# A graph layer and a feed-forward layer on one core: the second phase written out, and a new order of work where the phases meet

## The reference, cut to what matters

```python
# x: 10000 x 1024, src, dst: 5000 edges
xn   = layernorm(x)
h    = xn @ W.T + b
deg  = 1 + count(src)
out1 = x + deg**-.5 * sum over row's edges of deg[dst]**-.5 * h[dst]   # and the row itself
z    = layernorm(out1)
base = z @ base_W.T + base_b
low  = (z @ shared_A.T) @ shared_B.T
gate = softmax(z @ router_W.T + router_b); the top 2 of 6, normed to sum 1
low += sum over experts of gate_e * (z @ routed_A[e].T) @ routed_B[e].T     # rank 16
out  = out1 + base + low
```

## Time and profile before

| | |
|---|---|
| median of 3 runs | 2042.78 us (2038.26 to 2043.79) |
| the profiled execution, its time | 2044.74 us |
| the profiled execution, its span | 2043.0 us |
| busy: PE, DVE, POOL, ACT | 95%, 72%, 46%, 44% of the span |
| mean granted TensorE clock | 0.987 |

### The profile page before, as it was taken

The page is one execution under the profiler, slowest core; times in us unless marked ns, Lnnn a source line. Parts: engine busy times, 40 slices in busy tenths (PEclk is TensorE's granted clock), DMA queues, the critical chain, the costliest instruction groups (busy, mean ns, idle before and its releaser), DMA issues.

```text
span 2043.0 us, 31611 instructions
## 1 busy us (share of the span) xinstructions
PE 1935.7 (95%) x9583; PEld 1613.6 (79%) x9583; DVE 1466.5 (72%) x3526; ACT 908.7 (44%) x1533; POOL 937.5 (46%) x964
## 2 busy tenths in 40 slices
PE   7999999999999999947999999999999999999999
PEld 6778777777787888836878878788888878888887
DVE  6878888888776777755666767677767767776775
ACT  4455555555555555534333333333334333343342
POOL 1712444444424500146555555555555555555550
PEclk9999999999999999979999999999999999999999
DMA  6524455455444453474323333333333333333321
GB/s 245 213 101 153 163 187 175 160 185 179 160 151 144 148 166 145 155 248 118 82 73 102 105 82 95 91 98 104 103 82 92 102 87 100 103 101 84 94 60 61
DMA packets 148959, 260.20 MB, mean 127 GB/s; under 512 B 56077, under 2 KB 75357, under 8 KB 148822
## 3 DMA queue, kind: packets, MB, share of 16 engines
q1 hardware_dynamic: 99478, 237.85, 33.2%
q0 software_dynamic: 49344, 20.85, 8.0%
HBM read 273.80 MB, written 129.74 MB: 198 GB/s over the span
## 4 chain that ended last, share of the span: by engine, by line
issue 35%; PE 28%; POOL 21%; DVE 10%; ACT 2%; DMA 2%; POOLq 0%; DVEq 0%; SPq 0%; ACTq 0%
POOL acc L863 8%; PE bo L1537 4%; PE bo L1541 4%; PE bo L1539 4%; POOL piece L832 2%; POOL counted L799 2%; PE bo L1397 2%; PE bo L1401 2%; PE bo L1399 2%; POOL xpw L741 2%; POOL pw L948 2%; POOL counts L813 2%; POOL slots L820 2%; DVE acc L2161 2%; POOL tick_pool L716 1%
## 5 line engine op out<-in xcount | busy, mean ns | idle before, releaser
L863 POOL DMA_INDIRECT acc<-h_rows,row_now x312 | 505.5, 1620 | 111.6 <-issue 111.1
L1397 PE MATMUL bo<-wr_hi,left_hi 128*128 128x512 f32 x1008 | 400.1, 397 | 4.5 <-ACT bo L1149 3.1
L1401 PE MATMUL bo<-wr_hi,left_lo 128*128 128x512 f32 x1008 | 394.0, 391 | 0.0
L1399 PE MATMUL bo<-wr_lo,left_hi 128*128 128x512 f32 x1008 | 393.4, 390 | 0.0
L741 POOL TENSOR_TENSOR xpw<-xpin,neg_half 128x1 f32<-128x1 f32 x79 | 72.6, 919 | 491.5 <-DVE xpin L1705 491.5
L1537 PE MATMUL bo<-wr_hi,sum_hi 128*128 128x512 f32 x624 | 249.2, 399 | 9.2 <-DVE acc L2161 7.2
L1539 PE MATMUL bo<-wr_lo,sum_hi 128*128 128x512 f32 x624 | 244.5, 392 | 0.0
L1541 PE MATMUL bo<-wr_hi,sum_lo 128*128 128x512 f32 x624 | 244.2, 391 | 0.0
L1397 PEld LDWEIGHTS bo<-wr_hi,left_hi 128*128 128x128 f32 x1008 | 189.8, 188 | 42.6 <-issue 5.7
L1401 PEld LDWEIGHTS bo<-wr_hi,left_lo 128*128 128x128 f32 x1008 | 189.7, 188 | 40.1
L1399 PEld LDWEIGHTS bo<-wr_lo,left_hi 128*128 128x128 f32 x1008 | 190.0, 189 | 37.1
(11 more groups left out here) (231 smaller groups left out, 4275.8 us busy)
## 6 DMA issues: line engine op xcount, KB each, us to landing
xn<-x SPq DMA_DIRECT2D x79, 512.0 KB, 3.9
r_rows<-xn SPq DMA_DIRECT2D x79, 512.0 KB, 2.6
acc<-r_rows SPq DMA_DIRECT2D x79, 512.0 KB, 4.4
out<-acc SPq DMA_DIRECT2D x79, 512.0 KB
h_rows<-hrow SPq DMA_DIRECT2D x144, 256.0 KB, 3.9
acc<-h_rows,row_now POOLq DMA_INDIRECT x312
wr_raw<-w_t SPq DMA_DIRECT2D x16, 256.0 KB, 6.1
piece<-base_t SPq DMA_DIRECT2D x64, 64.0 KB, 2.8
```

Source lines behind the costliest of these rows:

```text
L863: nc.gpsimd.indirect_dma_start(to[:], None, h_dram, bass.IndirectOffsetOnAxis(ap=at, axis=0), bounds_check=NPAD - 1, oob_is_err=False, com ...
L1397: nc.tensor.matmul(ps, left_hi[n][:, k, :], wr_hi[n][:, k, :], start=False, stop=False, skip_group_check=True)
L1399: nc.tensor.matmul(ps, left_hi[n][:, k, :], wr_lo[n][:, k, :], start=False, stop=False, skip_group_check=True)
L1401: last = nc.tensor.matmul(ps, left_lo[n][:, k, :], wr_hi[n][:, k, :], start=False, stop=(k == 3), skip_group_check=True)
```

## The change

1. `pipeline` loses its loop: all 39 pairs are straight-line code on every engine.
2. GpSimd's `step`: `power(1,1)` first, then rounds (3,0), (2,3), (3,1), `power(2,0)`, (3,2); round (2,2) of the first pair goes ahead of the loop. Before: (2,2), power, (2,3), (3,0), power, (3,1).
3. At the seam, tiles 1 and 2 are filled by two chains: rounds 0 and 2 add into `acc`, rounds 1 and 3 go to a buffer `g_side` of their own, which VectorE adds before the statistics (`add_side`). Two memsets of `g_side` are new.
4. VectorE's lower parts of T1, B21, B22 move from ahead of the narrow weights' to places among the first tiles' steps; those of the low rows, T2, T3 and T4 shift too. ScalarE's high parts follow; the narrow one comes first.
5. In phase one `begin_second(0)` goes ahead of a norm and of `weigh(6)`, and T1's lower part behind the statistics of the first pair's second tile.
6. Some semaphores are merged (`zeroed`, `slots_set`), and waits on counts follow.

```diff
-SPLIT_AT = {B11: 4, T1: 8, B21: 12, B22: 16, "narrow": 17, "low": 18, "step": 19, T2: 23, T3: 27,
+SPLIT_AT = {B11: 4, "narrow": 5, T1: 9, B21: 13, "low": 14, B22: 18, "step": 19, T2: 23, T3: 27,
...
-def pipeline(eng, body, last):
-    a = DEEP
-    b = (PAIRS2 - 3) // DEEP * DEEP
-    for i in range(0, a):
-        body(Pair(i // DEEP, i % DEEP))
-    with eng.Fori(a // DEEP, b // DEEP) as k:
-        for q in range(DEEP):
-            body(Pair(k, q))
-    for i in range(b, last + 1):
+def pipeline(body, last):
+    for i in range(last + 1):
         body(Pair(i // DEEP, i % DEEP))
...
+        g_side = [sb(f"g_side{t}", [P, D], F32, w_end + 16 * HALF + 32 * HALF * t)
+                  for t in range(2)]
...
             for q in range(2):
                 nc.gpsimd.memset(g[q][:], 0.0).then_inc(g_zeroed, 1)
-            pool.wait_ge(g_zeroed, 3)
+            pool.wait_ge(done, product_at(PAIRS - 1, S3))
+            for t in range(2):
+                nc.gpsimd.memset(g_side[t][:], 0.0).then_inc(g_zeroed, 1)
+            pool.wait_ge(g_zeroed, 5)
...
+            def put_aside(t, r, at):
+
+                nc.gpsimd.indirect_dma_start(
+                    g_side[t][:], None, h_dram, bass.IndirectOffsetOnAxis(ap=at, axis=0),
+                    bounds_check=NPAD - 1, oob_is_err=False).then_inc(g_aside[t], 16)
...
             for t in range(2):
-                fill(0, t, 0, 0)
+                add_tile(z0, 0, t, 0, g_fill[t])
+                put_aside(t, 1, slot_of(t, 1))
             power(0)
             for t in range(2):
-                fill(0, t, 1, 32 + t)
-            for r in range(2, ROUNDS):
-                for t in range(2):
-                    fill(0, t, r, 30 + 2 * r + t)
-            power(1)
-            rest_in(z0, 1)
+                pool.wait_ge(g_fill[t], 16)
+                carry_wait(32 + 2 * t)
+                add_tile(z0, 0, t, 2, g_fill[t])
+                pool.wait_ge(g_aside[t], 16)
+                carry_wait(33 + 2 * t)
+                add_rows(g_side[t], slot_of(t, 3), g_aside[t])
+            rest_in(z0, 1)
+            carry_wait(36)
+            for t in range(2):
+                add_tile(z0, 1, t, 0, g_fill[t])
+            power(1)
...
+            round_of(z0, 2, 2, 48)
+
             def step(s):
                 c = 22 + 4 * (s.q % 2)
-                if s.has(2):
-                    added(s, 2, 1)
-                    carry_wait(c)
-                    add_pair(s, 2, 2)
                 if s.has(1):
                     power(s.tile(1, 1))
...
                     slots_of(s, 3)
                     rest_in(s, 3)
-                    carry_wait(c + 2)
-                    add_pair(s, 3, 0)
+                    round_of(s, 3, 0, c)
+                if s.has(2):
+                    round_of(s, 2, 3, c + 1)
+                if s.has(3):
+                    round_of(s, 3, 1, c + 2)
                 if s.has(2):
                     power(s.tile(2, 0))
                 if s.has(3):
-                    added(s, 3, 0)
-                    carry_wait(c + 3)
-                    add_pair(s, 3, 1)
+                    round_of(s, 3, 2, c + 3)
...
             sums_high(0)
+            begin_second(0)
             normalise(first(1))
             weigh(HEAD - 1)
-            begin_second(0)
...
-                if t == 5:
+                if t == HEAD - 1:
                     quarter_low(T1, wr_raw[T1], 4)
-                if t == HEAD - 1:
                     left_low(0, A11, a11[:])
...
-            right_low(T1)
-            right_low(B21)
-            right_low(B22)
             dve.wait_ge(rest_hi_ok, SPLIT_AT["narrow"])
...
             add_first()
             acc_statistics(0, 0)
             acc_scales(0)
-            low_rows_split()
+            right_low(T1)
             for v, n in ((0, A11), (1, A12)):
                 y_low(-1, n, bt[v][:])
-            z0 = Pair(0, 0)
-            right_low(T2)
+            right_low(B21)
+            low_rows_split()
+            add_side(0)
             pair_statistics(z0, 0, 0)
             acc_scales(1)
+            right_low(B22)
             choose(-1, 1)
             hidden(-1, 1)
+            y_low(0, A11, y11[:])
+            add_side(1)
             pair_statistics(z0, 0, 1)
             acc_scales(2)
-            y_low(0, A11, y11[:])
             hidden_low(-1, 1)
+            split_low("step", slice(2, 3))
+            right_low(T2)
             sums2(0, None)
             weighed_sum(0, 0, 0, first_bank[1][:], (low_done, 1))
             lows(0)
+            y_low(0, S2, y_raw[S2])
+            y_low(0, S3, y_raw[S3])
             weighed_sum(0, 0, 1, third_bank[1][:], (low_done, 2))
+            right_low(T3)
             pair_statistics(z0, 1, 0)
-            y_low(0, S2, y_raw[S2])
             acc_scales(3)
-            y_low(0, S3, y_raw[S3])
-            right_low(T3)
...
                 hidden(p, 2)
+                weighed_sum(s.acc(0, 1), s.tile(0, 1), 1, third_bank[q][:],
+                            (y_done, y_product_at(p, S1)))
                 if not s.has(-1):
                     right_low(T4)
-                weighed_sum(s.acc(0, 1), s.tile(0, 1), 1, third_bank[q][:],
-                            (y_done, y_product_at(p, S1)))
```

More of the change, by code:

```diff
@@ L393, in gnn_ffn @@
         g_fill = [sem(f"g_fill{t}") for t in range(2)]
+        g_aside = [sem(f"g_aside{t}") for t in range(2)]
         piece_in, piece_ok, piece_out = sem("piece_in"), sem("piece_ok"), sem("piece_out")
@@ L704, in _ @@
             load_right(T4)
-            pipeline(sp, step, PAIRS2)
+            pipeline(step, PAIRS2)
             for q in range(DEEP):
@@ L951, in _, with fill, slot_of @@
             z0 = Pair(0, 0)
[L952 to L958 removed]
+            def fill(t, r, n):
+                pool.wait_ge(g_fill[t], 16 * (2 + r))
+                carry_wait(n)
+                add_tile(z0, 1, t, r, g_fill[t])
+            def put_aside(t, r, at):
+                nc.gpsimd.indirect_dma_start(
+                    g_side[t][:], None, h_dram, bass.IndirectOffsetOnAxis(ap=at, axis=0),
+                    bounds_check=NPAD - 1, oob_is_err=False).then_inc(g_aside[t], 16)
+            def slot_of(t, r):
+                n = t * ROUNDS + r
+                return row_now[0][:, n:n + 1]
             carry_wait(14)
@@ L1272, in _ @@
                 .then_inc(rest_hi_ok, 1)
-            act.wait_ge(bl_step_ok, 1)
-            nc.scalar.activation(bl_hi[:, 2, :], bl_raw[:, 2, :], ACT.Copy).then_inc(rest_hi_ok, 1)
             def norm(n, a, *waits):
@@ L1341, in _ @@
                 y_high(-1, n, bt[v][:], (za_done, v + 1))
-            right_high(T2)
+            right_high(B22)
             act.wait_ge(y_done, 1)
             nc.scalar.activation(third_bank[1][:], first_bank[1][:], ACT.Copy).then_inc(y_begun, 1)
+            act.wait_ge(bl_step_ok, 1)
+            nc.scalar.activation(bl_hi[:, 2, :], bl_raw[:, 2, :], ACT.Copy).then_inc(rest_hi_ok, 1)
+            right_high(T2)
             narrow_out(-1, 1)
@@ L1375, in step @@
                     begin_second2(s.pair(1), s.mod(1, 2))
-            pipeline(act, step, PAIRS2 - 1)
+            pipeline(step, PAIRS2 - 1)
         @block.tensor
@@ L1685, in step @@
                 low(third_bank[q][:], 0, 1)
-            pipeline(pe, step, PAIRS2 - 1)
+            pipeline(step, PAIRS2 - 1)
         @block.vector
@@ L2074, in pair_statistics @@
                 if s.filled(a):
-                    dve.wait_ge(g_fill[t], 16 * ROUNDS * (s.pair(a) + 1))
+                    dve.wait_ge(g_fill[t], 16 * (2 + ROUNDS * s.pair(a)))
                 else:
@@ L2202, in low_rows_split, with add_side @@
                                         ALU.subtract).then_inc(bl_step_ok, 1)
-                for n, at in (("low", slice(0, 2)), ("step", slice(2, 3))):
-                    dve.wait_ge(rest_hi_ok, SPLIT_AT[n])
-                    dve.wait_ge(bl_step_ok, 1)
-                    nc.vector.tensor_tensor(bl_lo[:, at, :], bl_raw[:, at, :],
-                                            bl_hi[:, at, :].bitcast(F32), ALU.subtract) \
-                        .then_inc(rest_lo_ok, 1)
+                split_low("low", slice(0, 2))
+            def add_side(t):
+                dve.wait_ge(g_fill[t], 32)
+                dve.wait_ge(g_aside[t], 32)
+                a = z0.acc(0, t)
+                nc.vector.tensor_tensor(acc[a][:], acc[a][:], g_side[t][:], ALU.add) \
+                    .then_inc(first_added, 1)
+                dve.wait_ge(first_added, 4 + t)
+            z0 = Pair(0, 0)
             add_first()
```

62 lines of the change are left out of this document (30 added, 32 removed).

## The result

The kernel after takes 2004.89 us in the median of 4 runs (2003.83 to 2005.26), the kernel before 2042.44 in 4 runs beside it. The ratio is 0.9819, with a 95% interval from 0.9802 to 0.9836: faster by 1.6 to 2.0%. The prediction was 2001, from 1993 to 2016. The profiled execution of after took 2003.83 us, its span is 2001.6.

A forecast was written before the change was run, and what follows sets the result against it. TensorE was taken as the bound, so only its idle time could be won: 18.9 + 13.2 + 7.5 + 2.0 = 41.6 us off 2044.74 gives 2003.1, less 1.96 to the median, 2001; range 1993 to 2016.

The forecast's parts named there:

- The loop, 18.9: Phase-two register loop, pairs 4 to 35: seven returns cost about 2.7 us each; writing pairs out wins 18.9, at least 15.
- I take the whole 18.9 as gain: Phase-two loop: straight-line code was taken to cost nothing, so all 18.9 us at the returns counted as won.
- The early pairs, 13.2: Phase-two pairs 1 to 7: 13.2 us above the floor of 26.99 a pair, from late GpSimd powers, all go; at least 6.
- The two edits that I named: Early pairs: GpSimd's power first with alternating gather rounds, and the first pair's four chained rounds made two chains; for the 13.2.
- the last pairs speak for it: End of phase two: the last two full pairs, already straight-line, run at 26.99 us each, so straight-line code costs nothing.
- The seam, 7.5: Where the phases meet: 5.0 us left at the first S1 product plus 2.5 in pair 0; between 4 and 9.5.
- The tick: Seam: GpSimd's one-element operation, 6.75 us beside VectorE's string, should take 0.2 and end at 892.9, 6.5 earlier.
- the first fill, 6.0 us behind: Seam: the first fill starts 6.0 us behind the tick, at 898.9.
- Pair 0's term of 2.5: Pair 0 at the seam: its S4 product's 2.73 us wait for a sum shrinks as the order turns; 2.5 us taken.
- my theory: Seam: VectorE's whole string of two-input instructions holds GpSimd's tick to its end; 6 us smaller if one instruction only.
- The first phase, 2.0: Near phase one's start: of TensorE's stops of 3.2 and 3.1 us, 2.0 is won, from 0 to 4.5.
- Slower through the early `rest_in`: GpSimd's steady pairs: a late load ahead of round (2,3) costs time in some 36 pairs, 2055 at 1.5 beyond; chance 0.04.

The follow-up runs named there:

- the string with gaps: Kernel after, VectorE's twelve lower parts of T1, B21, B22 back ahead of the narrow one, each waiting for the one before: 2002.59 us.
- the string back: Kernel after, the twelve lower parts back ahead of the narrow one without pauses: 2003.3, 2009.9, 2009.4, 2008.0 us; repeated, 2009.0 to 2012.2.
- A22 first: Kernel after, ScalarE in phase one takes the next pair's A22 upper parts ahead of a normalisation and C21's weighing: 1980.54 us, ratio to before 0.9721.
- the pauses at the seam besides: Kernel after with the A22 move, plus the twelve lower parts back at the seam, each waiting for the one before: 1980.47 us, ratio to before 0.9719.

## Why the prediction was right, and where it was not

The sum was right: 41.6 us were forecast between the profiled executions, and it is 2044.74 - 2003.83 = 40.9. This is in part luck: the sum counts the losses of the stretches, which all went, while two of its steps name the wrong cause or the wrong size, as follows. The median is 3.9 above the forecast, since I took 1.96 off for the distance of the profiled run of before from its median, while that of after lies 1.06 under its own.

*The loop, 18.9.* The stretch from pair 8 to 38 gave 18.5, so the size is right. The step "I take the whole 18.9 as gain" of writing the pairs out names the wrong cause. Behind the new seam a return costs 1.1 us, so the loop is worth some 7.6 to 8.0 of it (6.9 in the medians). The other 11 us came from the seam, with which VectorE's second stop at each return went. And with the old seam, writing the pairs out costs 6 us and more. I had read L2170's "issue" and overlooked the row of L2152 under it, 11.1 us in the same 7 turns.

*The early pairs, 13.2.* It was 13.23. The two edits that I named are each enough behind the rest of the new seam: the old order has 188.90 us there, the new order behind the old chain 188.91. Without either, and with the old seam's string and long tick besides, the ring governs in six of seven runs. The old order and the old chain behind the rest of the new seam were not run together, so that rest may be enough by itself. That the loop ends the ring in before is argued, not shown: pairs 7 and 8, around the first return, take 31.2 and 29.2 us, in which GpSimd gets ahead, and pair 9 takes 26.99. The straight-line version has no pause at that place, and six of its seven runs stay in the ring. One long pair alone doesn't end it: there pair 28 took 30.7 us, pair 29 26.97, and from pair 30 to 35 it was 27.6 to 28.9 again. I had written of straight-line code that the last pairs speak for it. They could not: in the straight-line kernel that is in the ring the same last two pairs take 26.96 and 26.99 us as well.

*The seam, 7.5.* The idle time ahead of the first transposes fell by 5.1 us (forecast 5.5), 0.95 of it was lost again up to marker -1 (forecast 0.5), and from there to pair 1 it gave 4.6 (forecast 2.5): 8.7 in all. With the first phase's 0.9 that makes the 9.6 us by which pair 1 comes earlier (992.87 and 983.27). The tick went as forecast (it ended at 891.82, 892.9 forecast). The power came at 906.41 (906.7 forecast), but for another reason: GpSimd was free at 905.25, and VectorE's variance, at 906.32, was last, because the first addition began at 900.62, not 898.9. The step "the first fill, 6.0 us behind" the tick failed: it was 8.8 us. The three transfers into `g` took 5.1 us in the median from issue to landing, against 2.6 in before; that they now run beside more of the weights' loads is a guess. Pair 0's term of 2.5 measured 4.6, and so the whole was 1.2 too small. It is no firm size, though: from marker -1 to 1 the kernel with the old order has 63.64 us, and the one with the old order and the loop, the same up to there, 61.30. And the stop that I named, 2.73 us ahead of the S4 product, gave only 0.6: at that place TensorE now waits 2.12 us (at 965.75) for the hidden rows. The rest came from stops ahead of it.

*The tick.* That the string holds this tick stands: four times in profiles (6.75, 7.17, 7.12 and 2.39 us, each to the string's end), and the hold goes when the string is gone or has pauses. As a rule for any string my theory falls, by the 35 ticks above. The Trainium skill, "SBUF — State Buffer", section "Who interferes with whom", has the shared ports held for one whole instruction. The 35 ticks are near it: each ended behind the instruction into which it came or behind the next, after at most 1.17 us. So are the tick in the string with gaps (0.19 us) and the one that came within the string's first instruction (0.26 us). The four long ticks, which came in the third instruction, are not: there the measurement says otherwise. But before's tick of 0.26 us at 923.33 came in a third instruction too, so the place in the string doesn't decide it either. What does stays open.

*The first phase, 2.0.* The step failed: it is 0, at the lower bound. The stop did not shrink, it was divided. The 0.9 us by which the phase ended earlier is chance; in the kernels here with the same first phase as after it ended between 884.9 and 888.7.

*The rivals.* Slower through the early `rest_in`: it cost nothing. From 1172 to 1960 VectorE waits once for a landing, 0.8 us, and GpSimd once for a residual's load, 5.9 us, with no stop of TensorE over 0.2 us.

## What to carry to other kernels

When two parts of a pipeline hang on each other in a ring, a late start can keep it in a slower gait to the end, as six of seven runs of one kernel here; ask what lets it catch up before taking out a pause that costs time. The loss in a stretch says how much there is to win, not which edit wins it: here the same 18.5 us would have been credited to the loop, and only runs with one edit undone showed that the seam carried most. Where a small operation of GpSimd on the critical path falls beside a string of VectorE's two-input instructions, measure how long it takes: here it was held to the string's end at one place and for one or two instructions at all others. A pause of 0.1 us between them was enough at the first.

## What the runs showed of the hardware that I had not expected

- One small GpSimd operation was held 7.12 us behind twelve VectorE subtractions that started 0.60 us apart, and 0.19 us where they started 0.80 us apart; 35 others that came into strings of four, starts 0.60 us apart, took at most 1.17 us.
- The same loop body cost VectorE one stop of 2.5 us at a return in one program and two, of 2.4 and 1.8, in another, with three instruction packets at the return in place of two.
- The granted clock of the first 134 us wasn't the same in every execution of one code: with the string back it was 1.00 and 0.99 in two profiles, and with A22 first 1.00 and, with the pauses at the seam besides, 0.97.
